# Loading the first weight block of a Winograd LoRA kernel in halves of contraction, with its first transposes in two banks

## The reference, cut to what matters

```
x = x + x @ W0.T + 0.5 * (x @ A0[label]) @ B0.T
x = x + x @ W1.T + b + 2 * (x @ A1[slot]) @ B1[slot]
```

## Time and profile before

| | |
|---|---|
| median of 3 runs | 295.47 us (295.28 to 295.89) |
| profiled execution | 295.05 us |
| its span, first to last instruction | 293.3 us |
| TensorE busy | 288.7 us, 98% of the span |
| VectorE busy | 243.3 us, 83% |
| ScalarE busy | 153.5 us, 52% |
| granted TensorE clock, mean | 1.000 |

### The profile page before, as it was taken

The page is one execution under the profiler, slowest core; times in us unless marked ns, Lnnn a source line. Parts: engine busy times, 40 slices in busy tenths (PEclk is TensorE's granted clock), DMA queues, the critical chain, the costliest instruction groups (busy, mean ns, idle before and its releaser), DMA issues.

```text
span 293.3 us, 4452 instructions
## 1 busy us (share of the span) xinstructions
PE 288.7 (98%) x1335; PEld 236.1 (81%) x1335; DVE 243.3 (83%) x369; ACT 153.5 (52%) x270; POOL 30.9 (11%) x81
## 2 busy tenths in 40 slices
PE   7999999999999999999999999999999999999996
PEld 6888888888888888877878878878878878878875
DVE  3779997999999999999996797797798698695432
ACT  3574576879257537463553463373364355355120
POOL 0715600010000501000100100100100100100000
PEclk9999999999999999999999999999999999999999
DMA  5999620800006510094167076068068159013004
GB/s 178 321 296 318 107 38 7 139 1 2 0 0 109 98 27 1 6 150 149 29 114 203 22 125 192 17 104 218 4 109 210 16 101 233 6 36 144 0 1 145
DMA packets 100803, 29.17 MB, mean 99 GB/s; under 512 B 85548, under 2 KB 93996, under 8 KB 100788
## 3 DMA queue, kind: packets, MB, share of 16 engines
q1 hardware_dynamic: 100788, 28.99, 42.4%
HBM read 20.59 MB, written 8.39 MB: 99 GB/s over the span
## 4 chain that ended last, share of the span: by engine, by line
PE 97%; DMA 1%; DVE 0%; SPq 0%; issue 0%
PE bank L1200 93%; PE bank L1223 2%; DMA a<-in_L_cond_W 1%; PE bank L1445 1%; PE bank L1412 0%; SPq L273 0%; DVE y L719 0%; DVE a_hi L760 0%; DVE a L719 0%
## 5 line engine op out<-in xcount | busy, mean ns | idle before, releaser
L1200 PE MATMUL bank<-v_hi,lhs 128*128 128x512 f32 (+1 forms) x136 | 42.6, 378 | 0.0
L1200 PE MATMUL bank<-vt_hi,s_hi 128*128 128x512 f32 x96 | 37.3, 389 | 0.0
L1200 PE MATMUL bank<-vt_lo,s_hi 128*128 128x512 f32 x96 | 37.3, 389 | 0.0
L1200 PE MATMUL bank<-vt_hi,s_lo 128*128 128x512 f32 x96 | 37.3, 389 | 0.0
L967 DVE STREAM_TRANSPOSE xt<-raw 128x512 int32<-128x512 int32 x32 | 32.5, 1077 | 0.5 <-DMA raw<-in_x 0.4
L1200 PEld LDWEIGHTS bank<-v_hi,lhs 128*128 128x128 f32 x136 | 25.1, 188 | 4.8
L469 ACT ACTIVATE lhs<-xt 128x512 fp32r<-128x512 f32 x32 | 19.6, 626 | 13.0 <-PE bank L1200 12.7
L1200 PE MATMUL bank<-v_lo,lhs 128*128 128x512 f32 (+1 forms) x68 | 25.8, 380 | 0.0
L1200 PE MATMUL bank<-vt_hi,lhs 128*128 128x512 f32 x64 | 22.1, 406 | 0.0
L719 DVE TENSOR_TENSOR lhs<-xt,lhs 128x512 fp32r<-128x512 f32 x32 | 21.7, 686 | 0.3
L435 POOL CAST ac<-c_hi 128x128 fp32r (+1 forms) x16 | 7.2, 450 | 135.9 <-PE bank L1200 98.9
(11 more groups left out here) (170 smaller groups left out, 658.0 us busy)
## 6 DMA issues: line engine op xcount, KB each, us to landing
raw<-in_x SPq DMA_DIRECT2D x32, 256.0 KB, 4.9
out<-y SPq DMA_DIRECT2D x31, 256.0 KB, 2.6
n<-in_L_cond_W SPq DMA_DIRECT2D x16, 256.0 KB, 5.8
a<-in_L_cond_W SPq DMA_DIRECT2D x16, 256.0 KB, 5.1
a_raw<-in_L_cond_lora_A SPq DMA_DIRECT2D x8, 128.0 KB, 2.4
b_raw<-in_L_cond_lora_Bs SPq DMA_DIRECT2D x16, 64.0 KB, 2.1
e_raw<-in_L_cond_lora_Bs SPq DMA_DIRECT2D x32, 32.0 KB, 1.8
a_raw<-in_L_cond_lora_As SPq DMA_DIRECT2D x8, 64.0 KB, 2.5
```

What stands on the lines that cost most here:

```text
L1200: return nc.tensor.matmul(ps, lhsT, rhs, start=start, stop=stop, skip_group_check=more)
```

## The change

The w1 tiles keep the order of w1's own rows, `[P, HK, H]`: row block first, then 512 columns. `load_n` now brings 256 columns (half h) of a given set of row blocks, in pieces of 1 KB. The first two loads on SP are both of `n11`, columns 0 to 255: row blocks 2 and 3 first (`n11_in[0]`), then 0 and 1 (`n11_in[1]`). After them come `a11[0]`, `a11[1]`, columns 256 to 511 of `n11` in one load of 512 KB (`n11_in[2]`), the index loads, `a11[2]`, `a11[3]`. `n22`, `n12` and `n21` come in two loads of 512 KB each where four of 256 KB stood.

The first turn writes two banks: blocks 2 and 3 when `n11_in[0]` is there, then blocks 1 and 0. VectorE rounds the first half from its bank (`half_turned`), ScalarE the second; `b11_lo[0]` and `b11[0]` are made in two halves. VectorE rounds columns 256 to 511 of `a11[0]` ahead of the identity, and TensorE starts M1 with m = 2, 3, then 0, 1. The warm-up between turn and product is 3 transposes, not 5. `a_low(1, 3)` moves ahead of the output sums of batch 0; for the later batches it stands at the end of the batch before, which is the same place in the queue. Two semaphores are joined into one (`m72_done`), with the same waits.

```diff
+            load_n(n11, 0, 0, 0, n11_in[0], PAIR[1])
+            load_n(n11, 0, 0, 0, n11_in[1], PAIR[0])
             for j in range(HK):
-                load_n(n11, 0, 0, j, n11_in[j])
                 load_a(a11, 0, 0, j, a11_in[j])
-                if j == 2:
+                if j == 1:
+                    load_n(n11, 0, 0, 1, n11_in[2])
                     sp.dma_start(index[0:1, 0:B], ...)
...
-            dve.wait_ge(n11_in[0], 16)
-            tt(n11[:, 0, 0, :], n11[:, 0, 0, :], eye[:, :], ALU.add, n_eyed)
+            dve.wait_ge(n11_in[1], 16)
+            tt(n11[:, 0, 0:P], n11[:, 0, 0:P], eye[:, :], ALU.add, n_eyed)
+            dve.wait_ge(half_turned, 1)
+            nc.vector.tensor_copy(b11_hi[:, 0, sides[1]], FIRST_BANK[1][:, sides[1]]).then_inc(w1_hi_made, 1)
             for j in range(2):
+                dve.wait_ge(a11_in[j], 16)
+                if j == 0:
+                    a11_high(0, sides[1])
                 part = a11[:, j, P * j:P * j + P]
-                dve.wait_ge(a11_in[j], 16)
                 tt(part, part, eye[:, :], ALU.add, w0_eyed)
                 dve.wait_ge(w0_eyed, j + 1)
-                for part in sides if j == 0 else (slice(0, H),):
-                    nc.vector.tensor_copy(a11_hi[:, j, part], a11[:, j, part]).then_inc(w0_hi_made, 1)
-                b11_low(j)
+                a11_high(j, slice(0, H) if j else sides[0])
+                if j == 0:
+                    dve.wait_ge(w1_hi_made, 2)
+                    for h in range(2):
+                        tt(b11_lo[:, 0, sides[h]], FIRST_BANK[h][:, sides[h]], b11_hi[:, 0, sides[h]].bitcast(F32),
+                           ALU.subtract, w1_lo_made)
...
+            pe.wait_ge(n11_in[0], 16)
+            for t in (2, 3, 1, 0):
+                if t == 1:
+                    pe.wait_ge(n11_in[1], 16)
+                if t == 0:
+                    pe.wait_ge(n_eyed, 1)
+                last = nc.tensor.transpose(FIRST_BANK[t // 2][:, P * t:P * t + P], n11[:, t, 0:P], eye[:, :])
+                if t == 3:
+                    last.then_inc(half_turned, 1)
+            last.then_inc(turned, 1)
+            warm_up(3)
             vm1_high(0)
```

More of the change, by code:

```diff
@@ L65, in two_layer_lora_kernel @@
     a21 = big("a21", 14, F32)
[L66 to L69, removed]
+    n11 = at("n11", [P, HK, H], F32, 12 * SLOT)
+    n21 = at("n21", [P, HK, H], F32, 20 * SLOT)
+    n22 = at("n22", [P, HK, H], F32, 16 * SLOT)
+    n12 = at("n12", [P, HK, H], F32, 17 * SLOT)
     t1, t1_lo, t1_hi = big("t1", 3, F32), big("t1_lo", 3), big("t1_hi", 1)
@@ L160, in two_layer_lora_kernel @@
         index_in = sem("index_in")
-        n11_in = [sem(f"n11_in{j}") for j in range(HK)]
-        n21_in = [sem(f"n21_in{j}") for j in range(HK)]
+        n11_in = [sem(f"n11_in{j}") for j in range(3)]
+        n21_in = [sem(f"n21_in{j}") for j in range(2)]
         n22_in = [sem(f"n22_in{j}") for j in range(2)]
@@ L266, in _, with load_n @@
             w0_v = w0.rearrange("(b j p) (a i) -> p b j a i", b=2, p=P, a=2)
-            w1_v = w1.rearrange("(n t p) (b j k) -> p n t b j k", n=2, p=P, b=2, k=P)
+            w1_v = w1.rearrange("(n t p) (b k) -> p n t b k", n=2, p=P, b=2)
             def load_a(tile, a, b, j, there):
                 sp.dma_start(tile[:, j, :], w0_v[:, b, j, a, :]).then_inc(there, 16)
-            def load_n(tile, n, b, j, there):
-                sp.dma_start(tile[:, j, :, :], w1_v[:, n, :, b, j, :]).then_inc(there, 16)
+            def load_n(tile, n, b, h, there, rows=slice(0, HK)):
+                sp.dma_start(tile[:, rows, sides[h]], w1_v[:, n, rows, b, sides[h]]).then_inc(there, 16)
+            load_n(n11, 0, 0, 0, n11_in[0], PAIR[1])
+            load_n(n11, 0, 0, 0, n11_in[1], PAIR[0])
             for j in range(HK):
-                load_n(n11, 0, 0, j, n11_in[j])
                 load_a(a11, 0, 0, j, a11_in[j])
-                if j == 2:
+                if j == 1:
+                    load_n(n11, 0, 0, 1, n11_in[2])
                     sp.dma_start(index[0:1, 0:B], label0.rearrange("(o b) -> o b", o=1)).then_inc(index_in, 16)
@@ L281, in _ @@
             for h in range(2):
[L282 to L285, removed]
+                load_n(n22, 1, 1, h, n22_in[h])
+                load_n(n12, 1, 0, h, n12_in[h])
                 for j in range(2 * h, 2 * h + 2):
@@ L291, in _ @@
                 load_a(a22, 1, 1, j, a22_in[j // 2])
-            for j in range(HK):
-                load_n(n21, 0, 1, j, n21_in[j])
+            for h in range(2):
+                load_n(n21, 0, 1, h, n21_in[h])
             for j in range(HK):
@@ L385, in add_eye_n @@
             def add_eye_n(tile, j, made):
-                tt(tile[:, j, j, :], tile[:, j, j, :], eye[:, :], ALU.add, made)
+                part = tile[:, j, P * j:P * j + P]
+                tt(part, part, eye[:, :], ALU.add, made)
             def add_eye_a(tile, j, made):
@@ L407, in _ @@
             for j in range(HK):
-                pool.wait_ge(n22_in[j // 2], 32)
+                pool.wait_ge(n22_in[j // 2], 16)
                 add_eye_n(n22, j, n_eyed)
@@ L488, in b11_copy @@
             def b11_copy(j):
-                act.wait_ge(w1_lo_made, j + 1)
+                act.wait_ge(w1_lo_made, j + 2)
                 bank_copy(b11, j, TURN_BANK[j], w1_made)
-            for j in range(2):
-                b11_high(j)
-                b11_copy(j)
+            act.wait_ge(turned, 1)
+            copy(b11_hi[:, 0, sides[0]], FIRST_BANK[0][:, sides[0]], w1_hi_made)
+            for h in range(2):
+                act.wait_ge(w1_lo_made, h + 1)
+                copy(b11[:, 0, sides[h]], FIRST_BANK[h][:, sides[h]], w1_made)
+            b11_high(1)
+            b11_copy(1)
             act.wait_ge(w0_hi_made, 3)
@@ L691, in batch @@
                 if not final:
-                    act.wait_ge(m2_done, b + 1)
+                    act.wait_ge(m72_done, 2 * b + 2)
                     a_high(b + 1, 1)
@@ L751, in _, with a11_high @@
             dve.wait_ge(eye_steps, 2)
-            dve.wait_ge(n11_in[0], 16)
-            tt(n11[:, 0, 0, :], n11[:, 0, 0, :], eye[:, :], ALU.add, n_eyed)
+            dve.wait_ge(n11_in[1], 16)
+            tt(n11[:, 0, 0:P], n11[:, 0, 0:P], eye[:, :], ALU.add, n_eyed)
+            def a11_high(j, cols):
+                nc.vector.tensor_copy(a11_hi[:, j, cols], a11[:, j, cols]).then_inc(w0_hi_made, 1)
+            dve.wait_ge(half_turned, 1)
+            nc.vector.tensor_copy(b11_hi[:, 0, sides[1]], FIRST_BANK[1][:, sides[1]]).then_inc(w1_hi_made, 1)
             for j in range(2):
+                dve.wait_ge(a11_in[j], 16)
+                if j == 0:
+                    a11_high(0, sides[1])
                 part = a11[:, j, P * j:P * j + P]
-                dve.wait_ge(a11_in[j], 16)
                 tt(part, part, eye[:, :], ALU.add, w0_eyed)
                 dve.wait_ge(w0_eyed, j + 1)
-                for part in sides if j == 0 else (slice(0, H),):
-                    nc.vector.tensor_copy(a11_hi[:, j, part], a11[:, j, part]).then_inc(w0_hi_made, 1)
-                b11_low(j)
+                a11_high(j, slice(0, H) if j else sides[0])
+                if j == 0:
+                    dve.wait_ge(w1_hi_made, 2)
+                    for h in range(2):
+                        tt(b11_lo[:, 0, sides[h]], FIRST_BANK[h][:, sides[h]], b11_hi[:, 0, sides[h]].bitcast(F32),
+                           ALU.subtract, w1_lo_made)
+                else:
+                    b11_low(j)
                 a11_low(j)
@@ L1104, in batch @@
             def batch(b, first, final):
[L1105 to L1109, removed]
+                if not (first or final):
+                    dve.wait_ge(s_sum_made, 4 * b + 4)
+                    turn_next(b + 1, range(3))
                 dve.wait_ge(m6_done, b + 1)
@@ L1180, in batch @@
                     s_low(b + 1, 2)
+                if first:
+                    a_low(b + 1, 3)
                 quarter_out(C22, BANK_E, z_sum)
@@ L1207, in row_tile @@
                 return tile[:, j, P * m:P * m + P]
-            taken = ([(w1_made, j + 1) for j in range(HK)] + [(w1_made, HK + 1), (w1_made, HK + 2)]
-                     + [(t1_made, 1), (t1_made, 2)] + [(w1_made, HK + 3), (w1_made, HK + 4)]
-                     + [(t1_made, 3), (t1_made, 4)] + [(w1_lo_made, HK + 1)])
+            taken = ([(w1_made, j + 2) for j in range(HK)] + [(w1_made, HK + 2), (w1_made, HK + 3)]
+                     + [(t1_made, 1), (t1_made, 2)] + [(w1_made, HK + 4), (w1_made, HK + 5)]
+                     + [(t1_made, 3), (t1_made, 4)] + [(w1_lo_made, HK + 2)])
             def turn(tile, j, n, eyed=0):
@@ L1222, in turn @@
                         pe.wait_ge(n_eyed, eyed)
-                    last = nc.tensor.transpose(ps[:, P * t:P * t + P], tile[:, j, t, :], eye[:, :])
+                    last = nc.tensor.transpose(ps[:, P * t:P * t + P], tile[:, t, P * j:P * j + P], eye[:, :])
                 last.then_inc(turned, 1)
```

(21 more changed lines are left out.)

33 lines of the change are left out of this document (16 added, 17 removed).

## The result

| | median, us | range | profiled execution | its span |
|---|---|---|---|---|
| before, 6 runs | 295.68 | 295.26 to 297.42 | 295.05 | 293.3 |
| after, 6 runs | 298.92 | 296.41 to 300.51 | 296.41 | 294.0 |

The changed kernel is slower by 1.1%: ratio 1.0111, 95% interval 1.0087 to 1.0135. The forecast was 296.3 with a range up to 297.4. The profiled execution is the fastest of the six; the other five took 298.5 to 300.5. So its trace shows one part of the loss; the larger part needs the trace of a longer execution, which the first experiment has.

The account below looks back on a forecast made before the run. The prediction took `a11[0]`'s landing, then an unbroken TensorE queue, as the bound. A mark 1.03 us later less 0.16 for `a_low(1, 3)` gave +0.87 on 295.05, or 295.9; on the median's scale 296.3, range 295.3 to 297.4.

Parts of the forecast that it names:

- The landing of `a11[0]`: Start of kernel: moved from second to third load, it lands at 6.1 us instead of 5.03; chance of 5.8 to 6.7: 0.33.
- upper bound: Latest landing of `a11[0]`: 7.0 us, from the third load's 7.33 less 0.3 for larger pieces.
- the hole in the transfers: Near-stop between second and third landings, 2.3 us apart; blamed on that time or any third load, or on 512 B pieces.
- lower bound of 5.5: Earliest landing of `a11[0]`: issue at 1.83 us plus 3.7, the shortest issue-to-landing time of such a load.
- rival 1: First loads: the hole takes the third load, `a11[0]` lands at 6.7 to 7.0, +1.5 to +1.8 us, some 297.1; chance 0.25.
- Rival 4: Start of M1: after a longer pause TensorE runs first matmuls at half pace, 1.3 us on top, 297.6; chance 0.05.
- Fewer `warm_up` transposes fall in idle time: nothing: Between first turn and M1: removing warm-up transposes was claimed to cost nothing.
- VectorE between landing and mark: From `a11[0]`'s landing to the high by low matmuls (the mark): 1.75 us instead of 1.79, gaining 0.04.
- The first turn: Path over `n11` to M1: mark at 6.25 to 7.1 us, deciding only if `a11[0]` lands before 5.35, which was excluded.
- `a_low(1, 3)`: Batch 1's `u_product`: making this tile earlier cuts a 0.32 us step to 0.23, together saving 0.16 us.
- Pieces, layout, larger loads: Later w1 loads: savings from larger pieces and fewer issues are hidden, and larger loads cause no TensorE wait.

Follow-up runs that it names:

- the first experiment: The changed kernel run again with no edit, to trace a typical execution: 299.27 us against 295.30 for the kernel before, ratio 1.0128.
- the second experiment: The changed kernel with 11 warm-up transposes between first turn and M1 in place of 3: 297.28 us against 295.30 for the kernel before, ratio 1.0062.

## Why the prediction was wrong

The direction was right and the place was right; the size was a quarter of what came (+0.8 of +3.2 us), and the range did not hold it.

**The landing of `a11[0]`: mis-sized, and its upper bound wrong.** The prediction "I take 6.1" fits the profiled execution (6.02). But the traces of longer executions have 7.2 (twice) and 8.0, over the bound of 7.0. That bound was the landing of one load in one trace, 7.33, less 0.3 for smaller pieces; nothing in one execution shows how far such a landing spreads. It was also read late: the earlier trace rows give when the waiting engine began. By the landings in the same trace the third load is there at 7.16, the fourth at 7.88 and the fifth at 8.73, so the steps are 0.72 and 0.85 us, not 0.6 and 0.95, and smaller pieces promised less than was worked out. Of the two causes offered for the hole in the transfers, the small pieces fell: with 1 KB and 2 KB pieces the third load is as late. Holding the later loads back brings it to 5.45 and 5.74, near the lower bound of 5.5. The price by the second experiment, where the fall of the pace is gone, is 2.0 us where +1.03 - 0.16 stood in the sum. So rival 1, at +1.5 to +1.8, was the better half of the truth.

**TensorE's pace: a term left out of the sum.** This is the step that failed most. Rival 4 names it, the longer pause and the half pace behind it, and gives it a chance of 0.05 and a price of 1.3 us on top. It is no exception: the trace of the changed kernel's long execution, those with `a_low` put back and with `a11[0]` second all have it, and by the mean granted clock so do 10 of the 23 executions of these three kernels (0.993 or 0.994), against none of the 18 with 11 warm-ups. The kernel before shows another form of it once its pause is not filled. Its price was 1.55 us inside that trace. In the median 2.0 us go with the warm-ups, of which 1.4 are inside the span. It would fit that in the long executions without a recorded fall the full pace comes late, but no trace shows it. "Fewer `warm_up` transposes fall in idle time: nothing" is not safe as written: in the kernel before five of them are worth 2.6 us, while with the undone order two of them are worth next to nothing. The argument in the earlier trace rows was there, since the early transposes ran at half pace; what was not asked is how near the kernel stood to losing the full pace. The Trainium skill (TensorE: Matmul & The Clock Gate, Part 1) has the throttled state as the default that activity lifts; the runs agree, with pieces of 3.78 us in place of 2.09 where the warm-ups were taken out.

**VectorE between landing and mark: nearly right.** 1.75 was forecast, 1.56 to 1.57 measured in the four traces in which TensorE kept full pace up to the mark, 1.79 stood before. Where it did not, it was 1.83 (`a_low` put back) and 1.93 (the hold). The new wait for `b_lo` is there, 0.37 us. The high matmuls at + 0.46 are exact. The reordering gains 0.23, not 0.04: VectorE's operations start 0.21 us after one another though each is 0.28 to 0.29 long, so `b11_lo` starts 0.76 after the landing, where the sum of lengths had 0.88.

**The first turn: right.** `b11_hi` was ready at 5.70, in front of `a11[0]`, and did not decide.

**`a_low(1, 3)`: right.** The 0.32 us step is 0.22 or 0.23 in each trace that has the move. Where it was undone it is 0.26, and the stretch over the eight matmuls is 2.19 us against 2.04. So the move is worth 0.15 to 0.2, close to the 0.16.

**Pieces, layout, larger loads: right,** hidden, with the kernel that has them alone at 295.26.

**The sum of the loss.** 3.97 us in the median of the changed kernel's second six runs: 1.98 stay when the warm-ups hold the pace (late load), 1.99 go with them. By the spans of the runs (mean 296.9 with 3 warm-ups, 295.5 with 11) 1.4 of these are inside the span, the pace; 0.6 are outside it. **That last part stays open.** The time outside the span is 1.70 to 1.87 us in all runs of all kernels with 5 or 11 warm-ups, and 1.7 to 3.2 in those with 3 or none, also where the order of loads was undone and the trace shows full pace. What happens in it no row shows.

## What to carry to other kernels

A median that lies 2.5 us over the profiled execution says that the trace is of another case; profile again until a typical one is caught. The first transfers of this kernel are not equal: the second landed at 4.5 to 5.5, the third at 6.0 to 8.0. Count how many loads the first product needs. Going from two to three cost 2 us here, for 0.2 gained in VectorE's order. Where an engine's pace hangs on its activity, as TensorE's does here, filler work ahead of the first product is part of the critical path: price its removal, and any longer wait in front of it, as a possible loss of pace and not as idle time.

## What the runs showed of the hardware

- **The granted clock of the first microseconds is not what the column says.** In the long execution the stretch from 3 to 4 us has PEclk 1.00, yet transposes there start 0.21 us apart, the pace of the stretch at 10 to 11 us with PEclk 0.50 (four in 0.85 us); at full pace four take 0.44. Read the early pace off the steps from start to start. When the full pace comes differs from one execution to the next: the same five warm-ups behind the first turn took 0.71 us in the trace of the kernel before and 1.27 in the one with the early low part alone.
- **Pace is lost in two ways.** In the kernel before without its five transposes the slow pace of the start lasted until about 10.5 us. In the changed kernel's long execution M1 began at full pace after a pause of 1.9 us and lost it from about 9.4 (0.68 in the stretch from 9 to 10 us) to 12.8, while TensorE was busy. With a pause of 0.86 us (the first trace) it kept it.
- **The third load of the kernel landed at 6.0 to 8.0 us, whatever it carried,** against 5.4 to 5.9 when no fourth is issued until it, or the second, is in.
